# Interpolation weights of a deformable convolution kept in fp32, turned three taps at once and spread from separate row groups of the array

## What is computed

```python
om = lax.conv_general_dilated(x, om_kernel, (SH, SW), 'SAME', ...) + om_bias
off = om[..., :2 * DG * K].reshape(Bx, Ho, Wo, DG, K, 2)
mask = jax.nn.sigmoid(om[..., 2 * DG * K:]) * 2.0
py = gy + off[..., 0]          # gy, gx: the pixel plus the tap's place in 3 x 3
px = gx + off[..., 1]
...                            # val: bilinear reading of x at (py, px), zero outside
cols = (val * mask_t[..., None]).reshape(Bx, Ho * Wo, K * Cx)
out = jnp.matmul(cols, kernel) + bias
```

## Time and profile before

| | us |
|---|---|
| median of three runs | 1110.71 |
| lowest, highest | 1101.46, 1111.42 |
| the profiled execution | 1106.04 |
| its span, first to last instruction | 1103.9 |
| mean granted TensorE clock | 0.861 |
| third stage, from its first offsets to its last addition | 213 to 513.6 |

### The profile page before, as it was taken

One profiled execution on the slowest core, in us unless ns is written; L12 is line 12 of the kernel. 1 busy time (PEld: TensorE's weight loads), 2 busy tenths in 40 slices (PEclk: granted clock), 3 DMA queues, 4 the chain that ended last, 5 costly groups with the idle time before them and its releaser, 6 DMA issues.

```text
span 1103.9 us, 16691 instructions
## 1 busy us (share of the span) xinstructions
PE 915.6 (83%) x4266; PEld 546.5 (50%) x4266; DVE 682.5 (62%) x2383; ACT 507.3 (46%) x1030; POOL 441.7 (40%) x1234
## 2 busy tenths in 40 slices
PE   5674677759989988889999977888986668999998
PEld 5563455435555455555444445455654554444443
DVE  6886667445555564564688767776575545656642
ACT  2333344446554664463466644334351013666664
POOL 6566567602454345436444311355364322111100
PEclk9999756558798898999999977987697657999999
DMA  5500000000000000000000000000000000000000
GB/s 81 88 1 1 0 0 1 1 1 1 1 1 0 0 0 0 1 1 1 1 0 0 1 1 0 1 0 0 0 1 1 0 0 1 6 5 10 5 5 10
DMA packets 26352, 6.21 MB, mean 6 GB/s; under 512 B 24068, under 2 KB 26244, under 8 KB 26308
## 3 DMA queue, kind: packets, MB, share of 16 engines
q1 hardware_dynamic: 25684, 5.70, 3.0%
q10 hardware_dynamic: 624, 0.01, 0.0%
HBM read 4.65 MB, written 1.05 MB: 5 GB/s over the span
## 4 chain that ended last, share of the span: by engine, by line
PE 52%; DVE 13%; issue 7%; ACT 4%; POOL 2%; DVEq 0%; ACTq 0%; POOLq 0%; another core or an unknown queue 0%
PE banks L1485 9%; PE banks L1311 7%; PE banks L1192 6%; PE banks L1193 4%; PE banks L1123 3%; PE banks L1502 3%; PE banks L1509 2%; PE banks L1453 2%; DVE weighted L2043 2%; PE banks L1303 2%; DVE summed L2047 2%; DVE V L1769 2%; PE banks L1266 2%; PE banks L1299 2%; PE banks L1287 1%
## 5 line engine op out<-in xcount | busy, mean ns | idle before, releaser
L661 POOL TENSOR_TENSOR rstd<-vareps,neghalf 128x4 f32<-128x4 f32 x64 | 66.5, 1039 | 252.1 <-DVE vareps L1753 246.8
L992 ACT ACTIVATE scratch<-banks,b 128x512 f32<-128x512 f32 x224 | 143.3, 682 | 50.5 <-PE banks L1193 38.1
L1485 PE MATMUL banks<-scratch,W 128*64 128x512 f32 (+1 forms) x448 | 146.5, 643 | 3.4 <-DVE weighted L2043 3.0
L1938 DVE TENSOR_TENSOR scratch<-banks,XR 128x1024 f32<-128x1024 f32 x72 | 87.5, 1224 | 90.1 <-PE banks L1303 64.2
L1192 PE MATMUL banks<-VS,W_hi 128*128 128x512 f32 x240 | 115.0, 479 | 2.1 <-DVE X L2119 1.0
L1193 PE MATMUL banks<-VS,W_lo 128*128 128x512 f32 x240 | 100.6, 419 | 0.0
L2043 DVE SCALAR_TENSOR_TENSOR weighted<-banks,b,cwide 128x512 f32<-128x512 f32 x72 | 54.0, 750 | 73.0 <-PE banks L1485 71.0
L1769 DVE TENSOR_SCALAR V<-X,moments,rstd 128x64 f32 (+1 forms) x256 | 67.9, 329 | 38.1 <-POOL rstd L661 31.0
L1311 PE MATMUL banks<-scratch,region 128*64 128x256 f32 x576 | 87.9, 431 | 3.0 <-DVE scratch L1938 3.0
L1003 ACT ACTIVATE cwide<-banks 128x512 f32<-128x512 f32 x96 | 57.5, 599 | 64.8 <-PE banks L1502 64.4
L1192 PEld LDWEIGHTS banks<-VS,W_hi 128*128 128x128 f32 x240 | 48.8, 203 | 50.3 <-issue 25.8
(11 more groups left out here) (290 smaller groups left out, 1991.3 us busy)
## 6 DMA issues: line engine op xcount, KB each, us to landing
W<-in_L_ffn_W SPq DMA_DIRECT2D x3, 512.0 KB
X<-in_x SPq DMA_DIRECT2D x8, 128.0 KB, 4.1
out<-X SPq DMA_DIRECT2D x8, 128.0 KB, 2.0
cwide<-in_L_ffn_W SPq DMA_DIRECT2D x2, 256.0 KB
KC<-in_L_conv_kernel SPq DMA_DIRECT2D x2, 144.0 KB
W<-in_L_ffn_W SPq DMA_DIRECT2D x1, 256.0 KB
cwide<-in_L_ffn_w SPq DMA_DIRECT2D x2, 128.0 KB
Ko<-in_L_conv_w SPq DMA_DIRECT2D x1, 144.0 KB, 2.8
```

The source lines that it names most:

```text
L661: pool.tensor_tensor(rstd[:], vareps[:], neghalf[:], ALU.pow).then_inc(rstd_ready, 1)
L992: act.activation(hid[:, c % 4, :], bank[c % 2][:, :], ACT.Gelu, bias=b1[s][:, w:w + 1]).then_inc(h_ready, 1)
L1485: ins = pe.matmul(y, W2[s][:, w, :], hid[:, c % 4, :], start=opens, stop=closes, skip_group_check=True)
L1938: vec.tensor_tensor(S[:, k % 3], pair(p), xr, ALU.mult).then_inc(s_ready, 1)
```

## The change

The hats stay fp32; the bf16 parts, their tiles and steps are gone. `hats` has four groups of 32 columns for each row of three taps: y values 0 to 7, y 8 to 15, x 0 to 7, x 8 to 15, 24 used (three taps by eight) and 8 that ScalarE sets to zero once. One `turn` of four fp32 transposes takes three taps, one row of the 3 x 3, so that `HT` has the y halves on partitions 0 to 31 and 32 to 63 and x on 64 to 127. `spread_tap` makes three fp32 matmuls from these three groups of rows, into the pair of banks and bank 0. Taps are spread two ahead of their gather, across the border of blocks too (taps 9 and 10 are 0 and 1 of the next block). Offsets use bank 7, z tiles and spreads alternate the two pairs. Slots 1 and 2 are issued in two parts. On GpSimd `front` moves from the end of a block to the next one's start, behind the norm's power, and seg1 behind it. `weighted` and `summed`, tiles of other stages, become views of one tile.

```diff
 NB = 8
 TAPS = 9
 KEEP = PIX // 2 - 1
-PARTS = 3
-HAT = 2 * PARTS * IMG
+SIDE = 3
...
         offs = sb("offs", [P, NT, 2 * TAPS])
-        HB = [sb(f"HB{u}", [P, NT * TAPS, HAT], BF16) for u in range(2)]
-        HT = sb("HT", [HAT, 2, 2, BLK], BF16)
+        HT = sb("HT", [P, SIDE, BLK])
         XR = sb("XR", [P, 3, BLK])
         S = view(scratch, 0, (3, 2, BLK))
         Z = [view(region, u * NT * TAPS * C, (NT, TAPS * C)) for u in range(2)]
...
-                    if s == 2 or first_half and s == 1:
+                    if s == 1 and first_half:
...
+                        front()
+                    if s != 1 and first_half:
                         seg1(step)
+                    if u == 0 and s == 2:
+                        rewind()
+                        split_later(i, s, wrap)
                     if first_half:
                         seg2(step)
                     if second_half:
                         seg3(step)
                     if second_half:
-                        if not (s == 5 and wrap):
+                        if s == 0 or s == 2 and wrap and u == 1 or s in (1, 5) and not wrap:
                             front()
                         rewind()
-                    if u == 0 and s in (2, 6):
+                    if u == 0 and s == 6:
                         split_later(i, s, wrap)
 
             def split(hi, raw, lo, first=None):
...
 
                 act.wait_ge(ht_psum, g + 1)
-                act.activation(HT[:, slot, 0:taps, :].rearrange("r k n -> r (k n)"),
-                               bank[7][0:HAT, 0:taps * BLK // 2].bitcast(BF16), ACT.Copy).then_inc(ht_ready, 1)
+                act.activation(HT[:, row, :], bank[7][:, :], ACT.Copy).then_inc(ht_ready, 1)
 
             def xr_out(n, k):
                 act.wait_ge(xr_psum, n + 1)
...
+            def z_tile(v, t, p):
 
                 n = TAPS * C // 2
                 for h in range(2):
                     for j, kernel in enumerate((KC_hi, KC_lo)):
-                        ins = pe.matmul(pair(Z_PAIR[t])[:, h, 0:n], VS[v][:, t * P:(t + 1) * P], kernel[:, h * n:(h + 1) * n],
+                        ins = pe.matmul(pair(p)[:, h, 0:n], VS[v][:, t * P:(t + 1) * P], kernel[:, h * n:(h + 1) * n],
                                         start=(j == 0), stop=(j == 1))
                 ins.then_inc(z_psum, 1)
 
-            def turn(k0, taps, v):
-
-                for j in range(taps):
-                    for t in range(NT):
-                        ins = pe.transpose(turned_hats(j)[:, t * P:(t + 1) * P], HB[v][:, t * TAPS + k0 + j, :], identb[:])
+            def turn(row, v):
+
+                for t in range(NT):
+                    ins = pe.transpose(bank[7][:, t * P:(t + 1) * P],
+                                       hats[v][:, SIDE * t + row, :, :].rearrange("p a r -> p (a r)"), ident[:])
                 ins.then_inc(ht_psum, 1)
 
-            def spread_x(k, slot):
-                pe.matmul(bank[0][:, :], spread[:, 2, :], HT[:, slot, k % 2, :], start=True, stop=True).then_inc(xr_psum, 1)
-
-            def spread_y(k, slot, p):
-                for h in range(2):
-                    ins = pe.matmul(pair(p)[:, h, :], spread[:, h, :], HT[:, slot, k % 2, :], start=True, stop=True)
-                ins.then_inc(yr_psum, 1)
+            def spread_tap(row, j, p):
+                quads = ((slice(0, QUAD), pair(p)[:, 0, :]), (slice(QUAD, 2 * QUAD), pair(p)[:, 1, :]),
+                         (slice(2 * QUAD, 4 * QUAD), bank[0][:, :]))
+                for q, (rows, out) in enumerate(quads):
+                    ins = pe.matmul(out, spread[rows, j, :], HT[rows, row, :], start=True, stop=True)
+                    if q:
+                        ins.then_inc((None, yr_psum, xr_psum)[q], 1)
 
             def gather(n, k, v):
 
...
-                        spread_y(k, (5 * u + k // 2) % 2, pairs[k])
-
-                    def x_of(k):
-                        pe.wait_ge(ht_ready, g + (k // 2 + 1))
+                        z_tile(v, t, (u + k) % 2)
+
+                    def spread_on(k):
+
+                        pe.wait_ge(ht_ready, g + (k // SIDE + 1))
                         pe.wait_ge(xr_ready, n + k)
-                        spread_x(k, (5 * u + k // 2) % 2)
-
-                    def turn_pair(p):
-                        pe.wait_ge(ht_ready, g + p)
-                        turn(2 * p, 1 if p == 4 else 2, u)
-
-                    turn_pair(1)
...
+                        pe.wait_ge(s_ready, n + (k - 2 + 1 + 3))
+                        if more and k in (3, 5, 7, 9):
+                            pe.wait_ge(z_copied, z + (k - 1) // 2)
+                        spread_tap(k // SIDE % SIDE, k % SIDE, (u + k) % 2)
+
                     pe.wait_ge(block_done, b + (NB * s + CREDIT))
                     gather(n, 0, u)
-                    slot1(step, bank[6])
-                    tap(2)
-                    turn_pair(2)
-                    x_of(3)
+                    spread_on(2)
+                    slot1(step, bank[6], 0)
+
+                    if more:
+                        z_next(0, 1)
                     gather(n + 1, 1, u)
-                    if more:
-                        z_next(0, 1)
-                    tap(3)
-                    x_of(4)
+                    slot1(step, bank[6], 1)
+                    spread_on(3)
+
                     gather(n + 2, 2, u)
-                    tap(4)
-                    turn_pair(3)
-                    x_of(5)
+                    spread_on(4)
+                    pe.wait_ge(ht_ready, g + 2)
+                    if more:
+                        pe.wait_ge(emask_ready, b + 2)
+                    turn(2, u)
+
+                    if more:
+                        z_next(1, 3)
                     gather(n + 3, 3, u)
-                    if more:
-                        z_next(1, 3)
-                    tap(5)
-                    x_of(6)
                     pe.wait_ge(ch_act, step * 3 + 3)
                     if u == 0:
                         prep(i * 2 + 2 - wrap, s_next, 0)
                     elif not wrap:
                         prep(i * 2 + 3, s, 1)
+                    spread_on(5)
+
                     gather(n + 4, 4, u)
-                    tap(6)
-                    turn_pair(4)
-                    x_of(7)
+                    spread_on(6)
+                    pe.wait_ge(vt_ready, b + (NB * s + 3) if more else NB * s + NB + 1)
+                    slot2(step, bank[6], 0)
+
+                    if more:
+                        z_next(2, 5)
                     gather(n + 5, 5, u)
-                    if more:
-                        z_next(2, 5)
-                    pe.wait_ge(vt_ready, b + (NB * s + 3) if more else NB * s + NB + 1)
-                    slot2(step, bank[6])
-                    tap(7)
-                    x_of(8)
+                    slot2(step, bank[6], 1)
+                    spread_on(7)
+
                     gather(n + 6, 6, u)
-                    tap(8)
-                    if more:
-                        pe.wait_ge(hb_ready, i * 4 + 2 * (u + 2))
+                    spread_on(8)
+                    if more:
                         pe.wait_ge(hb_done, b + 2)
-                        pe.wait_ge(ht_ready, g + 5)
-                        turn(0, 2, v)
+                        pe.wait_ge(ht_ready, g + 3)
+                        turn(0, v)
+
+                        z_next(3, 7)
                     gather(n + 7, 7, u)
                     slot3(step, bank[6])
                     if more:
-                        z_next(3, 7)
-                        pe.wait_ge(ht_ready, g + 6)
-                        pe.wait_ge(xr_ready, n + TAPS)
-                        spread_x(0, (5 * u + 5) % 2)
-                        pe.wait_ge(s_ready, n + (TAPS + 3))
-                        spread_y(0, (5 * u + 5) % 2, TAP_PAIR[0])
-                        pe.wait_ge(xr_ready, n + (TAPS + 1))
-                        spread_x(1, (5 * u + 5) % 2)
+                        spread_on(9)
+                        turn(1, v)
+
                     gather(n + 8, 8, u)
                     if not wrap:
                         pe.wait_ge(vp_ready, b + 3)
-                        pe.wait_ge(z_copied, z + NT)
+                        pe.wait_ge(ht_ready, g + 5)
                         offsets(u)
-                        pe.wait_ge(omt_ready, b + 3)
+                    if more:
+                        spread_on(10)
                     pe.wait_ge(yt_ready, b + 1)
                     turn_output(bank[1][:, PIX:2 * PIX])
                     if not wrap:
+                        pe.wait_ge(omt_ready, b + 3)
                         turn_offsets()
 
...
 
-            def hats_masked(b):
+            def hats_masked(b, v):
                 vec.wait_ge(hat_made, b + 1)
                 settle()
-                link(vec.tensor_tensor(hats[:, 0], hats[:, 0],
...
-                hb = HB[v][:].rearrange("p n (a r) -> p a n r", a=2)
```

(21 more changed lines are left out.)

282 lines of the change are left out of this document (125 added, 157 removed).

## The result

The changed kernel takes 1211.2 us (median of 4 runs, 1209.7 to 1211.8) against 1111.1 for the kernel before (4 runs, 1101.5 to 1112.2): ratio 1.093, 95% interval 1.088 to 1.099. It is 9% slower; the forecast was 1086, the range ended at 1158. The profiled execution has a span of 1208.9 us against 1103.9, so 105.0 us have to be found.

The account below looks back on a forecast made before the run. TensorE, working 83% of the span, was taken to set the pace. A gain of 16.9 us in the third stage, 21.9 with the prologue, gave 1084, or 1089 by the median; it said 1086, range 1070 to 1158.

Parts of the forecast that it names:

- The spreads: On TensorE, a tap's three fp32 spread matmuls overlap fully: +0.30 us a tap, +2.7 us a block of nine taps.
- The bounds of a tap: A tap's three spreads on TensorE: 0.97 us if all overlap, 2.85 us if none do.
- the open point: Whether 32-row tiles overlap beside a 64-row one on TensorE; the trace had only 64-row tiles side by side.
- I take 1.05: Spread time of a tap on TensorE, in us, with 0.04 for a third set of weights.
- Turns: TensorE's transposes in a block: 36 bf16 ones at 2.4 us become 12 fp32 ones at 2.2, no difference.
- Waits: TensorE's waits in a warm block: spreading two taps ahead leaves 0.8 of 3.8 us.
- The clock: TensorE's clock in the third stage: all blocks warm; if not, each of three blocks costs up to 5.9 us more.
- ACT, VectorE, GpSimd: Less copying and subtracting on these engines, none over 20.35 of 32.8 us a block; earns only in the prologue.
- Prologue: Ahead of the third stage's blocks: first gather at 239.4 instead of 244.42, gain 5 us, bounds 0 and 8.
- The sum of the stage: Third stage's blocks: seven of 32.5 us and a last of 24.8, 252.3 against 269.2, a gain of 16.9.
- The first rival: On TensorE the 64-row spread waits for the 32-row pair: +1.30 us a tap, 1149 to 1154; chance 0.33.
- Nothing overlaps: A tap's three spreads on TensorE run one after another: 2.85 us a tap, 1205 in all; chance 0.04.

Follow-up runs that it names:

- e1: Changed kernel with all three spreads as 64-row tiles, in the order first half of y, x, second half of y: 1132.5 us.
- e2: Changed kernel with x spread from 32 rows only, so all three spreads have one shape; output not the reference's: 1100.4 us.
- e5: Changed kernel with a tap's x weights on 16 neighbouring rows, so all three spreads are 32-row tiles; output the reference's: 1104.6 us.
- e7: Changed kernel with only VectorE's addition to X moved ahead of the product of the next block's second tap: 1168.6 us.
- e9: As e1, but with x last, behind both halves of y: 1148.7 us.
- e4: Changed kernel with each of the three spreads as a matmul over all 128 rows, zeros in the constant elsewhere: 1213.9 us.
- e10: Changed kernel with the edits of e4 and e7 together: 1194.1 us.
- e6: As e5, with VectorE's addition to X moved ahead of the product of the next block's second tap: 1083.6 us.
- e8: As e6, with the spread of the block's third tap ahead of the border wait and first gather on TensorE: 1082.8 us.

## Why the prediction was wrong, point by point

**The spreads: this step failed.** The bounds of a tap, 0.97 and 2.85 us, held the 2.11, and the text named the 64-row tile beside 32-row ones as the open point. The step that failed is "I take 1.05, nearest to the earlier trace rows". Those rows show two tiles of one shape; the 0.31 us of the last bf16 spread ahead of a gather in the earlier trace rows, where the shape changes, spoke for a wait, and it was priced at 0.09. e1, e2 and e5 show what decides: tiles on other rows overlap, in fp32 and threefold, if they have the same shape (1.06 us), and not if they differ (2.11). The Trainium skill (TensorEngine Tiling (Array Packing), Key Properties) says that changing the tiling mode, and not only the tile, drains TensorE; after's rows agree, with 2.11 against 1.06, and show that rows which nothing else uses don't escape it. For a block, measured: 31.0 of work (busy in e5, where 31.5 were summed), 7.8 for the shape (38.8 in e7; 9 x 1.05 less 2 x 0.76 of slot work beside x are 7.9), 1.0 idle and 4.6 of the clock, 44.4. In all seven, from gather to gather: after would take 276.2 us at full clock (6 x 39.8 and a seventh without offsets, 37.4), before 225.6 (6 x 32.8 and 28.8), 50.6 more; the rest of the 308.1 and 248.3 is the clock, 31.9 and 22.7, 9.2 more; together 59.8.

**Turns:** taken as about equal, 2.2 for 2.4 us a block. They are cheaper: twelve fp32 transposes take 1.4 us in after (0.41, 0.41 and 0.59, from 391.92, 407.36 and 412.37), 0.8 less, and the rest of a block came out 0.5 under the sum.

**Waits: the old ones right, a new one missed.** XR's waits and that for the offsets are gone, and 1.0 us a block is idle where 0.8 was said. But it is another wait. The changed order on VectorE (products two taps ahead) puts a product of 1.22 us between the turn of the output and the addition to X, and the gather behind it is the first instruction of the block. It could be read in the new order: which instruction stands on VectorE between `yt` and the addition.

**The clock: failed.** "I therefore take all blocks as warm" was an argument without a row. After has 0.88 in seven blocks and 0.52 in the last, which takes 50.3 us where e7's, at full clock, takes 28.6. Even with the overlap as forecast (e5) it was 0.88 in the stage, which costs up to 33 us of 273.4 (0.12 of it). In four pairs that differ in the border's idle time (stages of e1 and e9, e4 and e10, e5 and e6, after and e7) the missed wait costs 5 to 9 us by itself and 9 to 22 through the clock. With 32-row tiles that was most of what the clock took. In the changed kernel it was a third: some 53 us of its stage are the clock's (119 us at half clock, about 0.45 lost of each), and e7, without the idle stretches, still loses some 36 of 333. What makes TensorE's clock fall there, with the engine busy, stays open.

**ACT, VectorE, GpSimd:** right, none of them binds. VectorE has 21.7 and ScalarE 34.6 us less work; it earned nothing.

**Prologue: the term was mis-sized.** Forecast 239.4 for the first gather, measured 243.4. The sum had one spread at 1.9 and 2.0 for XR and the product. Ahead of the gather stand two spreads, each 4.0 us at the half clock that runs there, and a turn of 1.0 between them. In e5 a spread takes 2.0 there and the first gather comes at 238.1.

**The rest of the program:** no term for it. It took 16.8 us more in after with the same matmuls, and the clock is the likely cause: after has 204 us at half clock there and before 154, since the half clock of the last block goes on to 628 and falls of later stages shift. The edits of the change to those stages are no rival: e5 has them too and takes 589.7, before 590.3.

**The sum of the stage:** it was too high even at full clock. It took seven whole blocks of 32.5 and a last one of 24.8. But the first piece of before in the earlier trace rows ends ahead of its border and the seventh block has no offsets, so before at full clock is 6 x 32.8, 28.8 and 20.9, 246.5 us, and not 7 x 32.8 and 23.7, 253.3. That e6 comes to 1083.6, near the 1086, is therefore luck in part: its stage is 243.2 where 252.3 were summed, and what follows takes 7 us more than before.

**The rivals.** The first rival was the case: its mechanism, place and mark (the third matmul about 1 us after the first, no waits of the spread for XR) are what the trace shows. Its price, 1149 to 1154, was too low by 60, as it too had the clock at 1.00 and no border wait; e7, without that wait, comes to 1168.6. With a sound weight on the shape change it should have been the likeliest. "Nothing overlaps" was not the case; its 2.85 us tap was nearly measured in e4, 2.77.

## What to carry to other kernels

Before relying on matmuls side by side, look at whether neighbouring tiles have the same shape (here they differed in rows; a difference in columns was not tried): give all of them one, even if that means rearranging data or leaving rows empty, and put small matmuls of that shape next to them. When the order of one engine is changed, read what now stands ahead of the instruction that ends a block, for a wait of 1 us there cost one to three times as much again here, through TensorE's clock. And price a stage at the clock that its rows show, not at full clock, until a run shows otherwise.

## What the runs showed of the hardware that was not expected

- Three fp32 matmuls of 32 rows on three row groups take 1.06 us together, one on the whole array 0.95. With 64-row tiles it made no difference which two ran together: x beside the first or the second half of y, 1.82 to 1.91 us a tap in e1 and e9 alike.
- An idle stretch of 1.0 to 2.1 us at a border, on a TensorE that was busy for over 30 us, was followed by the half clock at 7 of 7 borders in after and e9, 6 of 7 in e5, 5 of 7 in e2 and e4; one of 0.27 to 0.51 us at none (six of e1, and the last ones of e6, e7, e10). The long ones without a fall were 1.08 (e2, e5), 1.18 and 2.11 (e4), 2.00 (e2) and 1.27 us (e1) long, so the length alone doesn't decide. Before has idle stretches at its borders too: the half clock came 1.3 to 2.3 us behind the three of 0.85 us (ended by the offsets' copy) and behind none of the three of 0.77 us, a difference so small that something else in those blocks may count.
- TensorE ran at half clock with no idle time at all for up to 24 us (e7) and 47 us (after, 553 to 600), with spreads of 64 rows at a time; not so with 96 rows at once (e6 from 254 on, e8 from 245 on) or 128 (e10), nor in e1, which has 128 and then 64, one profile of each. Whether it is the rows in use that count, the data in them or the mix with the rest of the block, these runs don't tell.
- The same instructions behind the third stage took 589.7 to 607.1 us, by where the half-clock stretches fell. A gain of under 10 us in one stage of this kernel can be lost there, as that of e8 was.
